# A sandwich layer on one core: the loads of the first three token tiles move from SyncE's DMA queue to ScalarE's

## What the reference computes

```
x = x + layernorm(attention(layernorm(x), w_qkv, w_dense))       # causal, 32 query heads on 8 key/value heads, head size 128
x = x + layernorm(ffn(layernorm(x), w1, s1, w3, s3, w2, s2))     # silu(g) * u, 512 -> 1792 -> 512, block scales of 128x128
```

## Time and profile before

| | us |
|---|---|
| median of 3 runs | 1146.74 |
| lowest and highest | 1146.15, 1146.76 |
| the profiled execution: its time | 1146.33 |
| its span, first to last instruction | 1144.5 |
| PE busy | 1122.0 (98%) |
| DVE busy | 836.4 (73%) |
| ACT busy | 627.4 (55%) |
| POOL busy | 719.1 (63%) |

### The profile page before, as it was taken

The page is one execution under the profiler, slowest core; times in us unless marked ns, Lnnn a source line. Parts: engine busy times, 40 slices in busy tenths (PEclk is TensorE's granted clock), DMA queues, the critical chain, the costliest instruction groups (busy, mean ns, idle before and its releaser), DMA issues. The chain is left out here.

```text
span 1144.5 us, 17840 instructions
## 1 busy us (share of the span) xinstructions
PE 1122.0 (98%) x5512; PEld 942.4 (82%) x5512; DVE 836.4 (73%) x1987; ACT 627.4 (55%) x1350; POOL 719.1 (63%) x802
## 2 busy tenths in 40 slices
PE   9999999999999999999999999999999899999997
PEld 7888888888888888888888888888887677888885
DVE  5645454557898897888888888988678876666666
ACT  6432324236776776766767666766678632222225
POOL 7844447436765865856856758657884746666645
PEclk9999999999999999999999999999999999999999
DMA  6443555335466575475474664654420043333422
GB/s 224 138 157 147 185 204 185 148 126 182 128 199 214 158 239 163 137 267 169 142 256 132 197 214 148 217 188 137 153 78 1 11 123 106 116 106 96 120 65 97
DMA packets 154696, 173.76 MB, mean 152 GB/s; under 512 B 41776, under 2 KB 128496, under 8 KB 151280
## 3 DMA queue, kind: packets, MB, share of 16 engines
q1 hardware_dynamic: 154608, 172.68, 46.6%
HBM read 101.06 MB, written 71.57 MB: 151 GB/s over the span
## 5 line engine op out<-in xcount | busy, mean ns | idle before, releaser
L924 POOL TENSOR_SCALAR probs_long<-probs_long,rsum 128x896 f32<-128x896 f32 (+9 forms) x124 | 124.7, 1006 | 67.8 <-DVE rsum L1501 66.7
L1234 ACT ACTIVATE probs_long<-probs_long,negmax 128x896 f32<-128x896 f32 (+9 forms) x124 | 121.4, 979 | 46.9 <-DVE negmax L1495 46.5
L924 POOL TENSOR_SCALAR probs_short<-probs_short,rsum 128x416 f32<-128x416 f32 (+15 forms) x128 | 74.4, 589 | 115.5 <-DVE rsum L1501 114.9
L1771 PE MATMUL psS<-kT_hi,qT_hi 128*128 128x256 f32 (+8 forms) x384 | 133.5, 348 | 0.0
L1771 PE MATMUL psS<-kT_hi,qT_lo 128*128 128x256 f32 (+8 forms) x384 | 128.2, 334 | 0.0
L1771 PE MATMUL psS<-kT_lo,qT_hi 128*128 128x256 f32 (+8 forms) x384 | 128.1, 334 | 0.0
L1915 PE MATMUL psOY<-wd_hi,oT_hi 128*128 128x512 f32 x256 | 107.1, 419 | 0.4 <-DVE oT_lo L1430 0.4
L991 POOL TENSOR_SCALAR hidden<-mask,hr,hs 128x128 f32<-128x128 f32 x112 | 49.9, 456 | 85.8 <-DVE hr L1594 83.3
L865 POOL TENSOR_TENSOR qT_lo<-q_raw,qT_hi 128x512 fp32r<-128x512 f32 x64 | 91.3, 1427 | 19.7 <-ACT qT_hi L1218 19.7
L1915 PE MATMUL psOY<-wd_hi,oT_lo 128*128 128x512 f32 x256 | 100.4, 392 | 0.0
L1915 PE MATMUL psOY<-wd_lo,oT_hi 128*128 128x512 f32 x256 | 100.2, 391 | 0.0
(11 more groups left out here) (200 smaller groups left out, 3265.0 us busy)
## 6 DMA issues: line engine op xcount, KB each, us to landing
q_raw<-q_scr SPq DMA_DIRECT2D x64, 256.0 KB, 3.5
p_scr<-probs_long SPq DMA_DIRECT2D x24, 512.0 KB, 3.3
raw<-in_w_qk SPq DMA_DIRECT2D x10, 1024.0 KB, 5.7
p_scr<-probs_long SPq DMA_DIRECT2D x21, 448.0 KB, 3.1
probs_long<-p_scr SPq DMA_DIRECT2D x90, 96.0 KB, 3.0
q_scr<-cB SPq DMA_DIRECT2D x16, 512.0 KB, 2.6
q_scr<-cA SPq DMA_DIRECT2D x16, 512.0 KB, 2.8
raw_wd<-in_w_dense SPq DMA_DIRECT2D x8, 1024.0 KB, 8.5
```

Source lines behind the costliest of these rows:

```text
L924: nc.gpsimd.tensor_scalar(row, row, rsum[:, column(t, h)], 1.0, ALU.mult, ALU.mult).then_inc(p_ready, 1)
L1234: nc.scalar.activation(row, row, ACT.Exp, bias=negmax[:, column(t, h)], scale=-1.0, accum_out=lsum[:, column(t, h)]).then_inc(e_done, 1)
L1771: last = nc.tensor.matmul(dst, a, b, start=(start and k == 0), stop=(stop and k == len(terms) - 1), skip_group_check=resumed)
```

## The change

The loop that loads tiles 0, 1 and 2 moves to the head of ACT's list, and SP's list starts with the four weight blocks. The semaphores are the same ones.

```diff
+    EARLY = 3
...
-            load_x(0)
-            load_values_weight(0)
-            load_x(1)
-            for k in range(1, KT):
+            for k in range(KT):
                 load_values_weight(k)
-            for i in range(2, 5):
+            for i in range(EARLY, 5):
                 load_x(i)
             sp.dma_start(raw[1][:], w_v[1]).then_inc(wv1_in, 16)
...
+            for i in range(EARLY):
+                nc.scalar.dma_start(xt[:, i, :], x[i * P:(i + 1) * P, :]).then_inc(x_in[i], 16)
 
             act.wait_ge(const_ready, 1)
             nc.scalar.copy(half[:, 1:2], half[:, 0:1])
```

## The result

The changed kernel takes 1148.47 us in the median of 20 runs (1146.80 to 1150.07), the kernel before 1146.55 in the median of 20 (1145.22 to 1147.70). The ratio is 1.0017, 95% interval 1.0010 to 1.0023: slower by 1.9 us, just under the 0.2% that the prediction set as its bound for a difference, and above its range, which ended at 1148.2. Three traces of the changed kernel have times of 1150.07, 1149.85 and 1149.0, three of the kernel before 1146.33, 1146.61 and 1145.88.

The account below looks back on a forecast made before the run. The prediction took the start as latency-bound until about 13.2 us, then a queue of PE work. Four zero terms and +0.5 us for tile 0's delay gave 1147.2 us on the median of 1146.74, range 1146.0 to 1148.2.

Parts of the forecast that it names:

- the 0.2% that the prediction set as its bound for a difference: Whole kernel: about 0.2% (2.3 us) is what a measurement can tell from no change; slower by more had chance 0.05.
- its range: Whole kernel's forecast time: 1146.0 to 1148.2 us, around a predicted median of 1147.2.
- forecast 2.1: Start of ACT's list: the table load begins at about 2.1 us instead of 0.73, behind three issues; cost 0.
- The term for tile 2: DVE's 0.65 us wait for tile 2 at 9.60 shrinks or goes, but is absorbed: 0, at most -0.65 us.
- The sign: Whole kernel: slower, a sum of +0.5 us.
- The step that failed: Tile 0's load beside weight block 0: lands between 3.42 and 4.36, delay 0 to +0.94 us, taken as +0.5.
- The bound: Start-up loads: tile 0 lands at the latest with weight block 0, at 4.36, so at most +0.94 us.
- The rival that was given 0.06: the clock: PE idles at 6.4 us and falls to half rate until tile 2's turn: +4.4, total 1151.6; chance 0.06 including other hidden costs.
- the gap of 0.88 us at 13.20: Argument against the clock falling: PE idled 0.88 us ahead of tile 2's turn and its clock stayed at 1.00.
- its first term: Start-up loads: tile 0 delayed by sharing DMA engines with weight block 0, +0.5 us.
- The term for tile 1: Tile 1 lands at 5.77, ACT reaches it after 8.63; landing earlier or a few tenths later costs 0.
- the sum: Whole kernel: 0 + 0 + 0 + 0 + 0.5 = +0.5 us on the profiled execution, 1146.33 to 1146.8.

Follow-up runs that it names:

- e13: The kernel before, unedited, traced a second time; traced execution 1146.61 us, tile 2's turn at 14.30 us.
- e3: Against the kernel before: all loads on SyncE's one queue, alternating weight block 0, tile 0, block 1, tile 1 and so on; 1147.69 us, ratio 1.0009.
- e6: The kernel before with a shorter PE filler, 12 instead of 23 transposes ahead of tile 0's turn; 1148.23 us, ratio 1.0013.
- e7: The kernel before with tile 2 fifth in its one load queue, ahead of weight blocks 2 and 3; 1146.92 us, ratio 1.0004.
- e9: The kernel before with PE's turn of tile 1 ahead of weight block 1's matmuls instead of block 2's; 1146.55 us, ratio 0.9997.
- e14: The kernel before, unedited, traced a third time; traced execution 1145.88 us, tile 2's turn at 13.78 us.
- e4: Against the kernel before: only tile 0 on ScalarE's queue, the rest on SyncE's in the old order; 1148.25 us, ratio 1.0013.
- e5: The changed kernel with a longer PE filler, 43 instead of 23 transposes ahead of tile 0's turn; 1147.69 us, ratio 1.0010 to the kernel before.
- e1: The changed kernel again, no edit, for a second trace; 1148.50 us, ratio 1.0019 to the kernel before.
- e11: The changed kernel a third time, no edit, for a trace of its start; traced execution 1149.0 us, tile 0's statistics at 5.94 us.
- e8: The changed kernel with queues exchanged: four weight blocks on ScalarE's, all tiles on SyncE's; 1147.09 us, ratio 1.0008 to the kernel before.
- e2: The changed kernel with SyncE issuing nothing until tile 0 has landed; 1149.79 us, ratio 1.0024 to the kernel before.
- e12: The changed kernel with SyncE held until the identity matrix is made, at about 1.5 us; 1148.14 us, ratio 1.0017 to the kernel before.

## Why the prediction was wrong

**What held.** A delay of turn 2 reaches the end: over the sixteen traces that instant moved by 3.6 us, and the span less that instant only between 1129.9 and 1132.0. The first trace of the changed kernel kept its 3.46 to the end. The 2.1 us of other variation also mean that a single pair of traces can't show a difference of a few tenths in time: e13 has turn 2 1.1 us later than the first trace of before and a span only 0.3 longer. Tile 0's lateness is passed on in full: turn 2 is 9.72 to 9.74 us behind tile 0 in the four traces where tile 0 came late and the clock stayed up. ScalarE's three issues took 1.39 us, its table load began at 2.15 (forecast 2.1), and this cost nothing, as block 0 came far later. The term for tile 2 was 0, within 0.06 us (9.72 to 9.74 without its wait, 9.78 with it). The sign was right too.

**The step that failed: "it lands at the latest with block 0 ... 4.36", and so a term between 0 and +0.94, taken as +0.5.** It measured +2.43 to +2.54 in the three traces of the changed kernel. The bound counted the 0.52 MB of tile 0 and block 0. When tile 0's statistics began, 0.95 to 0.98 MB had been moved, 0.51 to 0.52 of them by SyncE's queue and 0.44 to 0.46 by ScalarE's; before it was 0.50. Three things are in it:

- Second place alone costs more than the bound. In e3, with one queue and nothing but the order changed, tile 0 is 1.45 late. The bound took block 0's landing from one trace (4.36); in the five other traces that load tile 0 and block 0 in this order (e6, e7, e9, e13, e14) ScalarE cast it at 4.41 to 4.77.
- Two queues at once cost more than the order. The bound pictured two transfers in flight, while each queue had its next ones running. In e4 the term is 1.68, and with tiles 1 and 2 behind tile 0 it is 2.3 to 2.5, e5 included. A load is whole when the last of its sixteen parts has landed, and the spread of these grew from 0.25 to 0.41 us in the three traces of before to 1.5 to 1.8 us.
- Issue at the same instant did not mean an even start. In the first trace ScalarE's packets came 0.5 us behind SyncE's, in e1, e4, e11 and also e8, where that queue carries the weights, 0.3 us. Alone (e2) or ahead (e12) its first ones come at 1.7 to 1.8 us, so it is the meeting with SyncE's issue that puts it second. With the queues exchanged (e8) tile 0 gets 1.0 us back, and with SyncE held 0.8 us (e12) it gets it all back.

The Trainium skill (DMA: Bandwidth & Descriptors, section "Issuing engines are not separate DMA queues") has it that transfers of several issuers interleave on the same engines. The trace agrees: both queues moved packets in every half microsecond from 2.0 us on, and the whole rate was hardly higher than with one queue (231 GB/s up to 8.2 us, 222 before). The prediction cited this rule and bounded its effect too low.

**The rival that was given 0.06: the clock.** The idle time ahead of turn 0 grew to 2.1 to 2.6 us and the clock fell to the lower level behind it, in all three traces of the changed kernel. The prediction argued from the gap of 0.88 us at 13.20, which costs no clock. That row said nothing on a gap nearly three times as long, which the prediction did not expect because its first term was too small. The price was also mis-sized, the other way: 1.07 us instead of 4.4, as the lower level had ended by 12.3 to 13.3 us, around the first product's matmuls and well ahead of tile 2's turn. The two errors belong together: in e3, e4 and e8 tile 0 is 1.4 to 1.7 us late, PE idles for 1.3 to 1.8, and the clock stays. The prediction also wondered that the granted clock read 1.00 over slow transposes; that was a stretch without a record.

**The term for tile 1, "landing a few tenths late costs nothing".** It looked at ScalarE's list only. On DVE the offset of tile 1 stands ahead of tile 0's low part. In the first trace of before it ran just in time for the 7.67 of the earlier trace rows; in e13, as in e9, tile 1 came 0.7 to 0.8 us later and turn 2 was late with it, by 1.1 us in e13. In e14 something else took 0.6 us: tile 0's turn itself ran for 1.06 us instead of 0.66, because the clock's rise came only at 7.7 us there (4.4 in e13, 6.0 in the first trace of before). In the changed kernel's three traces tile 1 never holds up DVE, since tile 0 is later still. This is why before's start is not as good as the one trace that the sum was made against.

**What stays open.** By three traces each the start accounts for 3.0 us; the medians differ by 1.9. The three traced executions of the changed kernel (1149.0 to 1150.07) lie in the upper part of its runs (1146.8 to 1150.07), those of before (1145.88 to 1146.61) in the lower. Whether tile 0 lands earlier in executions without a trace here was not seen. There is a sign that in some of them the clock did not fall. The mean granted clock of an execution reads 0.997 or 0.998 in the four traces with a fall, and 0.998 or 0.999 in those without. Of the 20 runs of the changed kernel eight read 0.999, with a mean time of 1147.6 us, and twelve 0.997 or 0.998, with 1148.9. In e1's runs the same division shows only 0.4 us, so this is a sign and not shown. Also open is why some parts of tile 0 fall behind when more stands behind it on its own queue. The times of the sixteen parts show that they do, not which engine held them or why.

## What to carry to other kernels

A second issuing queue is not a second path. What it takes away from the transfer that everything waits for is its place ahead of the others; look at what is in flight beside that transfer and behind it, and at which queue's packets come first, not only at when it is issued. A transfer is whole when its last part is, and the parts spread as more is in flight. When PE's filler transposes are sized to a latency, a longer latency can cost twice, once as itself and once as the clock behind the gap: here so at gaps of 2.1 us and more, and not at 1.8 and less. And one trace of a start-up phase is one draw: here the landing of the third transfer varied by 0.7 us and the clock's first rise by 3.3 us, and the apparent slack with them.

## What the runs showed of the hardware

- With both queues issued within 0.01 us of each other at 0.73 us, SyncE's packets began at 1.7 to 1.8 us and ScalarE's at 2.0 to 2.3, in five traces with tile 0 on ScalarE's queue and in e8 with the weights on it. With ScalarE's queue alone (e2) its packets began at 1.7 to 1.8, and its tile 0 landed by 3.49, as on SyncE's.
- The sixteen parts of one 256 KB load landed within 0.25 to 0.41 us of each other at the head of the only queue (3.07 to 3.40 in the first trace of before), within 0.83 us beside another queue (4.24 to 5.07, e4), and within 1.5 to 1.8 us with two more loads behind it on its own queue (4.09 to 5.83, changed).
- The rate can dip in the first microseconds: 156 and 147 GB/s in the two half microseconds from 3.7 us in the first trace of before, 193 in the microsecond from 4 us after, with 404 to 413 later. It does not in every trace: between 3.5 and 4.5 us it was 301 in e3, 336 in e4 and 326 in e6, which has the loads of before.
- PE idle for 2.38 us ahead of tile 0's turn had a granted clock of 0.51 from 9.20 to 12.20 us. The other traces with an idle time of over 2 us there (2.64 in e1, 2.14 in e11, 2.17 in e2) have the fall as well. Idle for 1.26, 1.39 or 1.79 us at the same place it kept the upper level: 13 transposes in 1.58 us.
- The first rise of the clock came between 4.4 and 7.7 us with the filler of 23 transposes or more, and at 10.7 us with 12. Ahead of it the trace has no record, and the column reads 1.00.
